# One-hot tables made in two halves, late squares held back, and a new order behind the search

## The chip, the cores and the metric

The kernel runs on one core of one Trainium2 chip. The metric is the device time of one execution in microseconds (us); the kernel before has a median of 389.44 us over 3 runs (389.33 to 390.71). A core has TensorE (PE, matmuls), VectorE (DVE), ScalarE (ACT), GpSimd (POOL) and SyncE (SP, which only issues DMAs here). Each engine runs its own instruction list in the order in which it is written; semaphores tie the lists together.

## The reference

1024 tokens (4 batches of 256) of width 256 pass through four residual blocks:

```
x = x + cross_attention(layernorm(x), ctx)                       # L0_xattn
x = x + turbo_ffn(layernorm(x), w_fc, w_proj)                    # L0_ffn
x = x + smooth_quant_experts(layernorm(x), fside, ctx)           # L1_xattn
x = x + product_key_ffn(layernorm(x), Wq, keys, e_down, e_up)    # L1_ffn

# turbo_ffn: the weights are quantised in blocks of 64. For each block 16 shrink factors are tried
# and the one with the least squared error is kept (the search); then relu(x wq_fc^T)^2 wq_proj^T
# smooth_quant (one expert per batch): s = sqrt(amax_x/amax_w); x/s and w*s rounded to int8 by row;
#   h = xq @ wq^T * scales; a = silu(gate) * up; then the same again with ctx as the down weights
# product_key_ffn: q = x Wq (4 heads, 2 halves of 64); per head and half sim = q keys^T, top 8 of 128;
#   top 8 of the 64 sums; index i1*128 + i2, clipped to the 2048 experts by the gather;
#   out = sum of silu(x . e_down[index]) * relu(score) * e_up[index]
```

## The kernel before, in words

**Stages.** The first 147 us are the search over the weights of the second block, 64 units of PE, ACT and DVE work, with the attention block between them. What the change touches lies behind it, from the line `pe.wait_ge(s["wT_e"], 6)` on in the list of TensorE and from the same place in the others. There, on four batches b (0 to 3) of two tiles of 128 tokens each (t = 2b + n, 0 to 7), these steps run:

- `ffn1(i)`, i = 8 to 15 (L590): the rest of the first feed-forward product; `relu(i)` on ACT (L1133) takes it out of PSUM and `square_hidden(i)` on GpSimd (L347) squares it. `ffn2(b, o)` (L736) is the second product, for batch b and output half o; it needs the transposed weights of chunk 2 or 3 (`w_transposed`, L578), and batches 2 and 3 need all sixteen squares. `x2(b)` on DVE (L1845) adds it to x and takes the statistics.
- The quantised expert (names with `c_`), for each batch a long chain between PE, DVE and ACT: `c_x_transposed`, `c_ratio`, `c_root`, `c_factor`, `c_diag`, `c_factors` (L753), `c_round` (L1875 and on), `c_integers`, `c_clip`, `c_quantised_transposed`, `c_first` (L777), `c_h` (L1902), `c_silu` (L1364), `c_a`, `c_a_transposed` (L784), and the same once more with names ending in 2, up to `c_second` (L813) and `x3(b)` (L1946, L1950). Batches 0 and 2 and 3 share PSUM bank 6, batch 1 has bank 7.
- `pre(b)` transposes the tokens; `half_queries` (L833) and `sims(b, n)` (L846) give the similarities; `experts(b, lo, hi)` (L862) computes the product of the tokens with all 2048 rows of e_down, in eight pieces a batch, which `gate` on ACT (L1418) takes out through silu.
- For each tile t, DVE finds the winners: `top8(t)` (L1960, L1966), `pair_top8(t)` (L1971 to L1981), `look_up(t)` (L1986 to L2002), which leaves for every token and slot the row and column of its expert and its coefficient in three bf16 parts, turned into `packT`. `mask(t)` (L2015) compares the row with 32 columns. `one_hots(t)` compares the column with 128 places (`oh`, L2022, 4096 elements a partition) and multiplies the mask with the three parts (`wc`, L2026, 3072 elements).
- `scatter(b, n, half)` (L884) multiplies `oh` with `wc`, 96 small matmuls for each half of 16 groups, into a dense table of coefficients in PSUM. For tiles 0 to 4 `coefficients_out` on ACT (L1410) moves it and `weigh` on GpSimd (L452) multiplies it with the gates; for tiles 5 to 7 `weigh` on DVE (L2044) does both. `up(b, n, lo, hi)` (L898), 16 pieces a tile, multiplies with e_up, and `result(t)` (L2050) adds it to x for the store.

**What sets the order.** Nothing but the written lists: the order of calls at the end of each engine's block. GpSimd's list is `ranks(t)` (L429), `coefficient_parts(t)` (L436 to L440) and `weigh`. Semaphore counts fix who waits for whom; `d_onehot` counts tiles, and `scatter` waits for it in its first half alone.

Of the kernel before, what the change touches and what calls it, by code (L numbers as in the profile page):

```python
# [36 lines left out]
def build(nc, x, ctx_1024, fside, wq0, bq0, wk0, bk0, w_fc, w_proj, wq1, keys, e_down, e_up, out):  # L37
# [23 lines left out]
    with ctx:  # L61
# [142 lines left out]
        def bk2(i):  # L204
# [16 lines left out]
            attT_t attT_e attn_t x1 ln1_var ln1_std ln1_inv ln1 ln2_var ln2_std ln2 x2T_t x2T_e edT_t edT_e  # L221
# [94 lines left out]
        def _(pool):  # L316
# [90 lines left out]

            square_hidden(8)
# [58 lines left out]
            weigh(2, (0, 1))  # L467
            ranks(4)
            weigh(2, (2, 3))
            coefficient_parts(4)  # L470
            weigh(3, (0,))
            ranks(5)
            weigh(3, (1, 2))
            coefficient_parts(5)
            weigh(3, (3,))
            weigh(4, (0, 1, 2))
            ranks(6)
            coefficient_parts(6)
            weigh(4, (3,))
# [5 lines left out]
        def _(pe):  # L485
# [418 lines left out]
            ffn1(8)  # L904
            ffn1(9)
            ffn1(10)
            pe.wait_ge(s["squared"], NU)
            gate_weights_transposed(0)
            pe.wait_ge(s["hsq"], 8)
            ffn2(0, 0)  # L910
            w_transposed(NCH - 1)
            ffn1(11)
            pe.wait_ge(s["wT_e"], 8)
            ffn2(0, 1).then_inc(s["f2_t"], 1)
            ffn1(12)
            ffn1(13)
            c_x_transposed(0)
            ffn2(1, 0)
            c_factors(0)
            ffn1(14)  # L920
            ffn2(1, 1).then_inc(s["f2_t"], 1)
            ffn1(15)
            c_row_scales(0)
            gate_weights_transposed(1)
            c_quantised_transposed(0)
            gate_weights_transposed(2)
            gate_weights_transposed(3)
            c_first(0)
            c_x_transposed(1)
            pe.wait_ge(s["hsq"], 16)  # L930
            ffn2(2, 0)
            c_a_transposed(0)
            ffn2(2, 1, (0,))
            c_factors(1)
            ffn2(2, 1, (1,)).then_inc(s["f2_t"], 1)
            c_factors2(0)
            ffn2(3, 0)
            ffn2(3, 1, (0,))
            c_row_scales(1)
            c_row_scales2(0)  # L940
            c_quantised2_transposed(0)
            c_quantised_transposed(1)
            c_second(0)
            c_first(1)
            ffn2(3, 1, (1,)).then_inc(s["f2_t"], 1)
            pre(0)
            c_a_transposed(1)
# [4 lines left out]
            c_factors2(1)  # L952
            experts(0, 0, 1)
            sims(0, 0)
            experts(0, 1, 3)
            c_row_scales2(1)
            c_quantised2_transposed(1)
            c_second(1)
            c_factors(2)
            experts(0, 3, 5)  # L960
            sims(0, 1)
            experts(0, 5, 6)
            pe.wait_ge(s["c_pre"], 3)
            pre(1)
            experts(0, 6, 7)
            pe.wait_ge(s["d_xT_e"], 2)
            c_row_scales(2)
            c_quantised_transposed(2)
            experts(0, 7, 8)
            c_first(2)  # L970
            scatter(0, 0, 0)
            c_a_transposed(2)
            half_queries(1, 0, 1)
            scatter(0, 0, 1)
            half_queries(1, 1, 2)
            experts(1, 0, 1)
            c_factors2(2)
            experts(1, 1, 3)
            sims(1, 0)
            experts(1, 3, 4)  # L980
            c_row_scales2(2)
            experts(1, 4, 6)
            c_quantised2_transposed(2)
            experts(1, 6, 7)
            c_second(2)
            experts(1, 7, 8)
            scatter(0, 1, 0)
            sims(1, 1)
# [9 lines left out]
            half_queries(2, 0, 1)  # L998
            up(0, 0, 8, 12)
            experts(2, 0, 1)  # L1000
            half_queries(2, 1, 2)
            up(0, 0, 12, 16)
            c_row_scales(3)
            sims(2, 0)
            c_quantised_transposed(3)
            experts(2, 1, 2)
            c_first(3)
            experts(2, 2, 3)
            scatter(1, 0, 0)
            c_a_transposed(3)  # L1010
            up(0, 1, 0, 4)
            experts(2, 3, 4)
            scatter(1, 0, 1)
            up(0, 1, 4, 16)
            c_factors2(3)
            experts(2, 4, 6)
            up(1, 0, 0, 4)
            c_row_scales2(3)
            sims(2, 1)
            c_quantised2_transposed(3)  # L1020
            up(1, 0, 4, 8)
            c_second(3)
            scatter(1, 1, 0)
            experts(2, 6, 8)
            up(1, 0, 8, 16)
            pre(3)
            scatter(1, 1, 1)
            half_queries(3, 0, 2)
            experts(3, 0, 1)
            scatter(2, 0, 0)  # L1030
            sims(3, 0)
            experts(3, 1, 2)
            scatter(2, 0, 1)
            up(1, 1, 0, 4)
            experts(3, 2, 3)
# [12 lines left out]
            scatter(3, 1, 0)  # L1048
            scatter(3, 1, 1)
            up(3, 0, 0, 16)  # L1050
# [4 lines left out]
        def _(act):  # L1055
# [97 lines left out]
            def square(g):  # L1153
# [7 lines left out]
                if g > QF_LATE:  # L1161
                    act.wait_ge(s["edT_t"], EROWS // 2)
# [256 lines left out]

            relu(8)  # L1420
            relu(9)
            relu(10)
            weights_out(NCH - 1)
            relu(11)
            std(0, 2, "ln3")
            relu(12)
            relu(13)
            c_root(0)
            c_diag(0)
            relu(14)  # L1430
            c_integers(0)
            std(1, 2, "ln3")
            c_row_scales_out(0)
            relu(15)
            c_integers_out(0)
            c_silu(0)
            c_root(1)
            c_diag(1)
# [752 lines left out]
```

## Time and profile before

| | |
|---|---|
| median of 3 runs | 389.44 us |
| the profiled execution's own time | 389.69 us |
| its span | 387.9 us |
| PE busy | 342.5 us (88%) |
| DVE busy | 343.1 us (88%) |
| ACT busy | 247.7 us (64%) |
| POOL busy | 99.6 us (26%) |

The span is the time from the first to the last instruction in the trace; the execution's own time has 1.8 us more around it. Busy time is the time in which an engine had an instruction under way. Two engines are busy for 88% of the span, and both have their idle time in other places, so that neither share alone says what a change in one stretch is worth.

### The profile page before, as it was taken

To read this page: it belongs to the slowest core of one execution; us is meant where nothing else is said; L and a number is where in the kernel's file an instruction comes from. 1 tells how busy PE (TensorE), PEld (TensorE's weight loads), DVE (VectorE), ACT (ScalarE), POOL (GpSimd) and SP (SyncE) were. 2 spreads that over 40 slices of the span, in tenths; PEclk is the share of its full clock that TensorE was granted. 3 is DMA by queue.
4 is the path that set the end of the run, shared out by engine and by line. 5 is a ranking of instruction groups with operands and counts; after the bars stand their busy time and mean duration, and the time that the engine had idled before them with its cause. 6 is when DMAs were issued, how large, how long until landed. Compare 5 with 4: busy or idle time off the path is not lost.

```text
span 387.9 us, 8250 instructions
## 1 busy us (share of the span) xinstructions
PE 342.5 (88%) x3222; PEld 250.7 (65%) x3222; DVE 343.1 (88%) x868; ACT 247.7 (64%) x371; POOL 99.6 (26%) x148
## 2 busy tenths in 40 slices
PE   2997898598968969999979889998999999989997
PEld 2454554144423425778978767887888887778876
DVE  4999999999999999368788999999999999999940
ACT  3899999979999982227457797755766654011000
POOL 3010011340660343121001104256424158601000
PEclk9999999869999999999989999999999999999999
DMA  8930000000000007100000000000000000000000
GB/s 254 358 132 2 1 0 2 1 1 0 2 1 0 2 0 235 37 0 3 0 2 0 3 0 3 1 3 2 0 18 14 2 15 4 2 15 2 18 15 27
DMA packets 11142, 11.40 MB, mean 29 GB/s; under 512 B 608, under 2 KB 10592, under 8 KB 11104
## 3 DMA queue, kind: packets, MB, share of 16 engines
q1 hardware_dynamic: 11104, 10.88, 8.8%
q8 instruction: 25, 0.41, 0.5%
q14 instruction: 13, 0.11, 0.1%
HBM read 9.83 MB, written 1.05 MB: 28 GB/s over the span
## 4 chain that ended last, share of the span: by engine, by line
DVE 53%; PE 25%; ACT 10%; issue 8%; DMA 2%; SPq 1%; POOL 0%; DVEq 0%; ACTq 0%
DVE arena L1627 10%; PE pair L898 7%; PE pair L736 5%; DVE i L1966 4%; DVE arena L1617 3%; DVE s L1960 3%; DVE arena L2026 3%; PE pair L590 3%; DVE arena L2022 2%; ACT arena L1167 2%; ACT arena L1164 2%; DVE XN L1552 2%; PE pair L884 2%; DMA arena<-in_L_ffn_keys_dram 2%; DVE pk L1981 2%
## 5 line engine op out<-in xcount | busy, mean ns | idle before, releaser
L1627 DVE TENSOR_REDUCE arena<-arena 128x16 f32<-128x1024 f32 x64 | 75.8, 1207 | 0.0
L862 PE MATMUL pair<-arena,EDT 128*128 128x256 f32 x256 | 60.2, 383 | 0.0
L898 PE MATMUL pair<-EU,arena 128*128 128x256 f32 x256 | 58.4, 382 | 0.6 <-DVE arena L2050 0.6
L898 PEld LDWEIGHTS pair<-EU,arena 128*128 128x128 f32 x256 | 47.9, 190 | 7.4 <-issue 1.0
L862 PEld LDWEIGHTS pair<-arena,EDT 128*128 128x128 f32 x256 | 47.1, 190 | 6.5 <-ACT arena L1418 0.2
L608 PE MATMUL pair<-arena,WQ 128*128 128x512 fp8e4 x112 | 35.8, 403 | 13.8 <-ACT arena L1164 8.8
L620 PE MATMUL pair<-arena 128*128 128x512 fp8e4 x128 | 40.5, 399 | 2.9 <-DVE arena L1617 2.9
L452 POOL TENSOR_TENSOR arena<-arena 128x512 f32<-128x512 f32 x20 | 27.4, 1383 | 45.0 <-ACT arena L1410 45.0
L1150 ACT ACTIVATE arena<-arena,clip_bias 128x1024 fp8e4<-128x1024 f32 x32 | 37.7, 1187 | 0.3 <-PE pair L620 0.3
L1164 ACT ACTIVATE arena<-pair,sq_bias 128x1024 f32<-128x1024 f32 x32 | 36.6, 1145 | 1.3 <-PE pair L620 1.3
L1418 ACT ACTIVATE arena<-pair 128x512 f32<-128x512 f32 x32 | 19.0, 598 | 26.4 <-PE pair L862 26.4
L1167 ACT ACTIVATE arena<-pair 128x1024 f32<-128x1024 f32 x32 | 33.6, 1051 | 1.4 <-PE pair L620 1.1
L347 POOL TENSOR_TENSOR arena<-arena 128x512 f32<-128x512 f32 x16 | 16.9, 1055 | 60.4 <-ACT arena L1133 60.4
L736 PEld LDWEIGHTS pair<-arena 128*128 128x128 f32 x256 | 30.7, 199 | 1.0 <-issue 1.0
L736 PE MATMUL pair<-arena 128*128 128x128 f32 x256 | 31.2, 282 | 0.0
L608 PEld LDWEIGHTS pair<-arena,WQ 128*128 128x128 bf16 x112 | 8.7, 101 | 34.3 <-ACT arena L1164 13.3
L590 PE MATMUL pair<-arena 128*128 128x512 f32 x64 | 29.7, 597 | 0.9 <-ACT arena L1126 0.7
L1410 ACT COPY arena<-pair 128x512 f32<-128x512 f32 x20 | 19.6, 1071 | 9.9 <-PE pair L884 9.9
L620 PEld LDWEIGHTS pair<-arena 128*128 128x128 bf16 x128 | 12.3, 102 | 20.2 <-issue 4.7
L884 PEld LDWEIGHTS pair<-arena 64*128 64x128 bf16 x1536 | 20.2, 93 | 6.5 <-issue 3.5
L884 PE MATMUL pair<-arena 64*128 64x32 bf16 x1536 | 21.7, 173 | 2.2 <-DVE arena L2044 1.3
L1617 DVE TENSOR_SCALAR arena<-arena 128x1024 fp8e4<-128x1024 f32 x32 | 22.2, 697 | 1.1 <-ACT arena L1138 1.1
(200 smaller groups left out, 642.6 us busy)
## 6 DMA issues: line engine op xcount, KB each, us to landing
arena<-in_L_ffn_e_down_dram SPq DMA_DIRECT2D x1, 2048.0 KB, 12.2
EU<-in_L_ffn_e_up_dram SPq DMA_DIRECT2D x1, 2048.0 KB, 9.3
arena<-in_L_ffn_w_fc_dram SPq DMA_DIRECT2D x2, 512.0 KB, 5.3
X<-in_x_dram SPq DMA_DIRECT2D x1, 1024.0 KB, 5.9
arena<-in_L_ffn_w_proj_dram SPq DMA_DIRECT2D x1, 1024.0 KB, 13.7
GUW<-in_fside_BxS2xS_dram SPq DMA_DIRECT2D x1, 1024.0 KB, 12.4
out_dram<-arena SPq DMA_DIRECT2D x8, 128.0 KB, 1.7
CTX<-in_ctx_dram SPq DMA_DIRECT2D x1, 512.0 KB, 4.8
```

Source lines behind the costliest of these rows:

```text
L590: last = pe.matmul(bank[2 + i % 2], W1T[:, k, m * P:m * P + P], xnT[:, k, half * 512:half * 512 + 512], start=(k == 0), stop=(k == 1))
L608: pe.matmul(to[half], stepN[:, j - 2, :], qr[:, (g - 2) % QDEEP, cols[half]], start=False, stop=False, skip_group_check=True)
L620: last = pe.matmul(to[half], stepI[:, j, :], qr[:, g % QDEEP, cols[half]], start=False, stop=True, skip_group_check=kept)
L736: last = pe.matmul(bk2(F2_BANK[b])[:, n, o * P:o * P + P], h2T[:, k, at:at + P], W2T[:, k, o * P:o * P + P], start=(k == 0), stop=(k == HI ...
L862: last = pe.matmul(bk2(4 + i % 2)[:, r, :], EDT[:, k, at:at + P], xT4[:, b % 2, k, :], start=(k == 0), stop=(k == 1))
L884: last = pe.matmul(bank[scatter_bank(t, half) + r][:, g16 * JW:g16 * JW + JW], oh[rows, g // NG, :, g % NG], wc[rows, c, g // NG, :, g % N ...
L898: last = pe.matmul(bk2(7)[:, n, :], PR[:, n, e, :], EU[:, e, :], start=(e == 0), stop=(e == EROWS - 1))
L1150: act.activation(qr[:, g % QDEEP, :], qu[:, g // NS % 2, :], ACT.Relu, bias=clip_bias[:, 0:1], scale=-GRID / STEPS[g % NS], saturate=False ...
L1164: act.activation(qd(g), pair[2 + g % 2][:, :], ACT.Square, bias=sq_bias[:, g % NS:g % NS + 1]).then_inc(s["squared"], 1)
L1167: act.activation(qd(g), pair[2 + g % 2][:, :], ACT.Square).then_inc(s["squared"], 1)
L1617: dve.tensor_scalar(qr[:, g % QDEEP, :], qu[:, g // NS % 2, :], TB_MAX * STEPS[g % NS], GRID / STEPS[g % NS], ALU.min, ALU.mult, saturate= ...
L1627: dve.tensor_reduce(err[:, g // NS % 2, :, g % NS], squares, AX.X, ALU.add).then_inc(s["reduced"], 1)
```

## The change

`one_hots(t)` becomes `one_hots(t, half)`. Each half makes 2048 elements of `oh` in one instruction and its half of `wc` in three, one for each part, of 512 elements; each half counts one up in `d_onehot`. `scatter` waits for its own half, `mask` for both halves of the tile before, and a half of `oh` waits only for the scatter of the same half of the tile before. On GpSimd `square_hidden(8)` and all after it wait for the last dequantisation, which is on DVE. The lists of PE, ACT, DVE and GpSimd behind the search are written in another order. One wait of `square` in the search is left out for four of five buffers, where an earlier wait covers it. The amount of work of PE, ACT and GpSimd is the same.

```diff
@@ GpSimd
+            pool.wait_ge(s["wquant"], NCH)
             square_hidden(8)
@@ GpSimd, behind ranks(0), coefficient_parts(0)
+            ranks(1)
+            coefficient_parts(1)
             weigh(0, (0, 1, 2))
-            ranks(1)
+            ranks(2)
             weigh(0, (3,))
-            coefficient_parts(1)
-            ranks(2)
-            weigh(1, (0, 1))
             coefficient_parts(2)
-            weigh(1, (2, 3))
+            weigh(1, (0, 1, 2, 3))
...
@@ scatter
-                if half == 0:
-                    pe.wait_ge(s["d_onehot"], t + 1)
+                pe.wait_ge(s["d_onehot"], 2 * t + half + 1)
@@ TensorE, behind ffn1(8)
-            ffn1(9)
-            ffn1(10)
             pe.wait_ge(s["squared"], NU)
-            gate_weights_transposed(0)
             pe.wait_ge(s["hsq"], 8)
             ffn2(0, 0)
+            ffn2(1, 0)
             w_transposed(NCH - 1)
-            ffn1(11)
+            gate_weights_transposed(0)
+            gate_weights_transposed(1)
             pe.wait_ge(s["wT_e"], 8)
             ffn2(0, 1).then_inc(s["f2_t"], 1)
+            ffn2(1, 1).then_inc(s["f2_t"], 1)
+            c_x_transposed(0)
+            ffn1(9)
+            ffn1(10)
+            c_x_transposed(1)
...
+            c_row_scales(1)
             c_first(0)
+            c_quantised_transposed(1)
+            c_first(1)
+            c_a_transposed(0)
+            c_a_transposed(1)
             pe.wait_ge(s["hsq"], 16)
             ffn2(2, 0)
+            c_factors2(0)
             ffn2(2, 1, (0,))
+            c_factors2(1)
+            ffn2(3, 0)
...
@@ TensorE, the end
             sims(3, 1)
-            up(1, 1, 4, 16)
-            scatter(2, 1, 0)
-            experts(3, 3, 5)
+            experts(3, 4, 6)
             scatter(2, 1, 1)
-            experts(3, 5, 7)
-            up(2, 0, 0, 4)
+            experts(3, 6, 7)
+            up(2, 0, 0, 16)
             experts(3, 7, 8)
-            up(2, 0, 4, 16)
             scatter(3, 0, 0)
             scatter(3, 0, 1)
             up(2, 1, 0, 16)
             scatter(3, 1, 0)
+            up(3, 0, 0, 4)
             scatter(3, 1, 1)
-            up(3, 0, 0, 16)
+            up(3, 0, 4, 16)
             up(3, 1, 0, 16)
@@ VectorE
-            def one_hots(t):
-
+            def one_hots(t, half):
+
+                o, k = slice(NO // 2 * half, NO // 2 * half + NO // 2), slice(16 * half, 16 * half + 16)
                 if t:
-                    dve.wait_ge(s["d_c_t"], 4 * t)
-                dve.tensor_tensor(oh, iotaI.unsqueeze(1).to_broadcast([P, NO, P, NG]), over(t, 1, P), ALU.is_equal)
+                    dve.wait_ge(s["d_c_t"], 4 * t - 2 + 2 * half)
+                column = packT[:, t % 2, 1, k].rearrange("p (o g) -> p o g", g=NG).unsqueeze(2).to_broadcast(
+                    [P, NO // 2, P, NG])
+                dve.tensor_tensor(oh[:, o], iotaI.unsqueeze(1).to_broadcast([P, NO // 2, P, NG]), column, ALU.is_equal)
                 dve.wait_ge(s["d_mask"], t + 1)
-                parts = packT[:, t % 2, 2:5, :].rearrange("p c (o g) -> p c o g", g=NG).unsqueeze(3).to_broadcast(
-                    [P, 3, NO, JW, NG])
-                dve.tensor_tensor(wc, msk.unsqueeze(1).to_broadcast([P, 3, NO, JW, NG]), parts, ALU.mult
-                                  ).then_inc(s["d_onehot"], 1)
+                for c in range(3):
+                    part = packT[:, t % 2, 2 + c, k].rearrange("p (o g) -> p o g", g=NG).unsqueeze(2).to_broadcast(
+                        [P, NO // 2, JW, NG])
+                    ins = dve.tensor_tensor(wc[:, c, o], msk[:, o], part, ALU.mult)
+                ins.then_inc(s["d_onehot"], 1)
@@ VectorE, the order of the expert stage
+            x2(1)
             c_ratio(0)
+            ln_apply(1, 2, "ln3")
             c_factor(0)
+            c_ratio(1)
+            c_factor(1)
             c_round(0)
+            c_round(1)
...
+            c_clip2(0)
+            c_clip2(1)
             x2(2)
...
@@ VectorE, the end
             top8(7)
+            pair_top8(7)
             weigh(5, (2,))
-            pair_top8(7)
+            one_hots(6, 0)
+            one_hots(6, 1)
             weigh(5, (3,))
-            one_hots(6)
+            result(4)
             look_up(7)
-            result(4)
-            weigh(6, (0,))
+            weigh(6, (0, 1, 2))
             mask(7)
-            weigh(6, (1,))
-            one_hots(7)
-            weigh(6, (2, 3))
+            one_hots(7, 0)
+            weigh(6, (3,))
             result(5)
+            one_hots(7, 1)
             weigh(7, (0, 1, 2, 3))
             result(6)
             result(7)
```

In the expert stage the lists of PE, ACT and DVE now take batches 0 and 1 side by side (`c_factors(0)`, `c_factors(1)`, `c_round(0)`, `c_round(1)` and so on) and batches 2 and 3 one after the other, where before each batch began some steps behind the last.

## Rows read from the trace of the kernel before

**Rows 1.** The page: busy time by engine, and the last chain's shares.

```profile
PE 342.5 (88%) x3222; PEld 250.7 (65%) x3222; DVE 343.1 (88%) x868; ACT 247.7 (64%) x371; POOL 99.6 (26%) x148
DVE 53%; PE 25%; ACT 10%; issue 8%; DMA 2%; SPq 1%; POOL 0%; DVEq 0%; ACTq 0%
```

**Rows 2.** Stretches: us, busy PE, PEld, DVE, ACT, POOL, PE clock, DMA, GB/s.

```profile
266.00:344.00 78.00, 74.95 (x1125) 64.38 (x1124) 75.46 (x243) 42.49 (x66) 33.98 (x38) 1.00 0.03 9
344.00:388.00 44.00, 40.16 (x632) 34.82 (x632) 28.72 (x66) 1.79 (x3) 1.43 (x6) 1.00 0.04 14
sum 244.00, PE 227.64 PEld 192.85 DVE 206.89 ACT 114.35 POOL 64.33; mean PE 22.76 PEld 19.29 DVE 20.69 ACT 11.44 POOL 6.43
```

**Rows 3.** The chain in order of time, its end (start, us, what).

```profile
342.13 2.08 DVE arena L2044 x2
344.26 1.37 PE pair L884 x96
...
351.01 1.73 PE pair L862 x8
...
378.10 7.16 PE pair L898 x32
```

**Rows 4.** Timeline, DVE: one-hot tables and their neighbours (start, us, line).

```profile
226.97 0.42 DVE L1993 TENSOR_TENSOR arena<-arena,i12f 128x512 bf16<-128x512 bf16 x1
...
229.19 0.69 DVE L2015 TENSOR_TENSOR arena<-arena,ctxT 128x1024 bf16<-128x1024 bf16 x1
...
229.80 0.42 DVE L1891 TENSOR_SCALAR arena<-arena 128x1024 bf16<-128x1024 bf16 x1
...
230.13 2.28 DVE L2022 TENSOR_TENSOR arena<-arena,ctxT 128x4096 bf16<-128x4096 bf16 x1
...
232.33 1.75 DVE L2026 TENSOR_TENSOR arena<-arena,ctxT 128x3072 bf16<-128x3072 bf16 x1
...
234.06 0.88 DVE L1902 SCALAR_TENSOR_TENSOR arena<-pair,rsc,arena 128x256 f32<-128x256 f32 x2
```

**Rows 5.** Timeline of GpSimd and DVE at 317 to 321 us: two together.

```profile
316.73 3.05 POOL L452 TENSOR_TENSOR arena<-arena 128x512 f32<-128x512 f32 x1 [3.38 <-ACT arena L1410]
...
318.56 2.83 DVE L2026 TENSOR_TENSOR arena<-arena,ctxT 128x3072 bf16<-128x3072 bf16 x1
```

**Rows 6.** Timeline of GpSimd and DVE at the last quantisation, and DVE's next stage.

```profile
149.24 1.04 POOL L347 TENSOR_TENSOR arena<-arena 128x512 f32<-128x512 f32 x1 [3.57 <-ACT arena L1133]
...
149.56 1.80 DVE L1595 TENSOR_TENSOR arena<-arena 128x1024 f32<-128x1024 f32 x1
...
162.17 0.69 DVE L1845 TENSOR_TENSOR X<-X,pair 128x512 f32<-128x512 f32 x1 [5.53 <-PE pair L736]
```

**Rows 7.** Timeline of PE, 181 to 202 us, the expert stage.

```profile
181.00 0.61 PE L777 MATMUL pair<-arena 128*128 128x256 bf16 x4 [0.22 <-ACT arena L1355]
...
181.88 3.74 PE L736 MATMUL pair<-arena 128*128 128x128 f32 x32
...
185.46 0.38 PE L784 MATMUL pair<-ident,arena 128*128 128x128 f32 x2
...
198.31 0.38 PE L800 MATMUL pair<-identb,arena 128*128 128x128 bf16 x4 [1.31 <-ACT arena L1390]
...
201.12 3.13 PE L736 MATMUL pair<-arena 128*128 128x128 f32 x16
```

**Rows 8.** Busy time by stretch, one us with the clock down.

```profile
201.00:202.00 1.00, 1.00 (x7) 1.00 (x6) 0.97 (x3) 0.00 (x0) 0.00 (x0) 0.50 0.00 0
```

**Rows 9.** Timeline: first similarities, first top 8, first scatter, second top 8.

```profile
211.68 1.16 PE L846 MATMUL pair<-keysT,arena 64*128 64x128 f32 x16
...
213.59 1.68 DVE L1960 MAX8 s<-pair 128x8 f32<-128x128 f32 x8
...
234.14 1.37 PE L884 MATMUL pair<-arena 64*128 64x32 bf16 x96
...
237.95 1.67 DVE L1960 MAX8 s<-pair 128x8 f32<-128x128 f32 x8
```

More of the change, by code:

```diff
@@ L908, in _ @@
-            gate_weights_transposed(0)
-            pe.wait_ge(s["hsq"], 8)
-            ffn2(0, 0)
-            w_transposed(NCH - 1)
+            c_x_transposed(1)
+            gate_weights_transposed(2)
+            gate_weights_transposed(3)
+            c_factors(0)
             ffn1(11)
-            pe.wait_ge(s["wT_e"], 8)
-            ffn2(0, 1).then_inc(s["f2_t"], 1)
+            c_factors(1)
             ffn1(12)
             ffn1(13)
-            c_x_transposed(0)
-            ffn2(1, 0)
@@ L919, in _ @@
-            c_factors(0)
+            c_row_scales(0)
             ffn1(14)
-            ffn2(1, 1).then_inc(s["f2_t"], 1)
+            c_quantised_transposed(0)
             ffn1(15)
[L923 to L927, printed above, removed]
+            c_row_scales(1)
             c_first(0)
-            c_x_transposed(1)
+            c_quantised_transposed(1)
+            c_first(1)
@@ L930, in _ @@
+            c_a_transposed(0)
+            c_a_transposed(1)
             pe.wait_ge(s["hsq"], 16)
             ffn2(2, 0)
-            c_a_transposed(0)
+            c_factors2(0)
             ffn2(2, 1, (0,))
-            c_factors(1)
+            c_factors2(1)
+            ffn2(3, 0)
+            c_row_scales2(0)
             ffn2(2, 1, (1,)).then_inc(s["f2_t"], 1)
[L936 to L940, printed above, removed]
@@ L941, in _ @@
             c_quantised2_transposed(0)
-            c_quantised_transposed(1)
+            c_row_scales2(1)
             c_second(0)
-            c_first(1)
-            ffn2(3, 1, (1,)).then_inc(s["f2_t"], 1)
+            c_quantised2_transposed(1)
+            ffn2(3, 1).then_inc(s["f2_t"], 1)
             pre(0)
-            c_a_transposed(1)
+            c_second(1)
             pe.wait_ge(s["d_xT_e"], 1)
@@ L951, in _ @@
             half_queries(0, 0, 2)
[L952 removed]
             experts(0, 0, 1)
+            c_factors(2)
             sims(0, 0)
[L955 to L962, printed above, removed]
+            experts(0, 1, 4)
             pe.wait_ge(s["c_pre"], 3)
             pre(1)
[L965 removed]
+            sims(0, 1)
             pe.wait_ge(s["d_xT_e"], 2)
             c_row_scales(2)
+            experts(0, 4, 5)
             c_quantised_transposed(2)
[L969 removed]
+            experts(0, 5, 6)
             c_first(2)
+            experts(0, 6, 8)
+            half_queries(1, 0, 2)
+            experts(1, 0, 1)
+            c_a_transposed(2)
+            experts(1, 1, 2)
             scatter(0, 0, 0)
[L972 to L973 removed]
+            experts(1, 2, 3)
+            sims(1, 0)
+            c_factors2(2)
+            experts(1, 3, 4)
             scatter(0, 0, 1)
[L975 to L980, printed above, removed]
+            experts(1, 4, 5)
             c_row_scales2(2)
[L982 removed]
+            experts(1, 5, 6)
             c_quantised2_transposed(2)
[L984 removed]
+            sims(1, 1)
             c_second(2)
[L986 removed]
+            experts(1, 6, 8)
             scatter(0, 1, 0)
[L988 removed]
             pe.wait_ge(s["x3"], 3)
@@ L1462, in _ @@
+            std(0, 2, "ln4")
+            tokens_out(0)
+            c_root(2)
             std(3, 2, "ln3")
+            queries(0, (0,))
+            c_diag(2)
+            queries(0, (1,))
             std(1, 2, "ln4")
-            gate(0, 3, 5)
+            gate(0, 0, 2)
             c_integers(2)
             tokens_out(1)
-            gate(0, 5, 6)
+            gate(0, 2, 4)
             c_row_scales_out(2)
-            gate(0, 6, 7)
             c_integers_out(2)
-            gate(0, 7, 8)
+            gate(0, 4, 8)
@@ L1472, in _ @@
             c_silu(2)
-            coefficients_out(0, (0, 1))
+            queries(1)
+            gate(1, 0, 1)
             c_root2(2)
-            queries(1, (0,))
-            coefficients_out(0, (2, 3))
+            gate(1, 1, 2)
             c_diag2(2)
-            queries(1, (1,))
-            gate(1, 0, 2)
+            coefficients_out(0, (0,))
+            gate(1, 2, 3)
+            coefficients_out(0, (1,))
             c_integers2(2)
-            gate(1, 2, 4)
+            gate(1, 3, 4)
@@ L1492, in _ @@
             queries(2, (0,))
-            gate(1, 7, 8)
             c_integers(3)
@@ L2115, in _ @@
             c_factor(3)
-            top8(3)
-            c_round(3)
             look_up(2)
             mask(2)
+            c_round(3)
+            one_hots(2, 0)
+            top8(3)
+            c_clip(3)
+            result(0)
             pair_top8(3)
-            c_clip(3)
-            one_hots(2)
+            one_hots(2, 1)
             c_h(3)
-            result(0)
-            c_a(3)
-            top8(4)
-            c_ratio2(3)
             look_up(3)
             mask(3)
+            c_a(3)
+            c_ratio2(3)
+            top8(4)
             c_factor2(3)
```

235 lines of the change are left out of this document (115 added, 120 removed).

## The prediction, made before the changed kernel was run

> **What bounds the kernel now.** I read the page first: PE and DVE are each busy for 88% of the span, and the chain that ended last gives 53% to DVE and 25% to PE [rows 1]. That is an average over stages, so the busy time by stretch came next. From 144 us, where the search ends for PE, to the end, PE is busy for 227.6 of 244 us [rows 2]. The last matmul ends at 378.10 + 7.16 = 385.26 us [rows 3], so 2.7 us of the 16.4 idle ones lie behind it, and 13.7 us is all that a new order can take from PE without taking work away. From 266 to 344 us PE has 3.0 us idle and DVE 2.5 [rows 2]: both are full at once, and a delay on either can reach the end.
>
> Third, the chain in order of time. Up to 344 us it runs on DVE; there PE waits for the multiplications of tile 5 (342.13 + 2.08), and from 344.26 us it is PE's own list to the end [rows 3]. So the end is set in two steps: DVE decides when PE can start that scatter, and what PE has left then decides the rest. What PE has left: 385.26 - 344.26 = 41.0 us. A change gains if DVE arrives at tile 5 earlier, or if PE has done more by then.
>
> **The hold, the search and GpSimd.** DVE's scaling at 149.56 takes 1.80 us; GpSimd's square runs until 149.24 + 1.04 = 150.28, so 0.7 us of it is waiting [rows 6]. With the squares held the last dequantisation should end about 2 us earlier (three such instructions). DVE then idles anyhow: its next stage starts at 162.17 after 5.53 us of waiting for PE [rows 6]. In the new order two second products stand ahead of PE's last weight transposition, about 7.2 us (32 matmuls take 3.74 and let the next start after 3.6 [rows 7]), so PE arrives there at about 155.5 us, when either version of the weights is ready. Gain on the path: 0, bounds 0 and 0.7 (one such wait). If this cover were gone, the 2 us would count in full, as a gain. The held squares are late by some us, but PE needs them only behind the first products of batch 2, 25 us later. The waits left out of the search cost an engine nothing that the trace shows: 0.
>
> **The halves.** The mask of 1024 elements starts at 229.19 and its neighbour at 229.80: 0.61 us. The table of 4096 goes from 230.13 to 232.33, 2.20 us, and the one of 3072 from 232.33 to 234.06, 1.73 us [rows 4]. So an element costs (2.20 - 0.61) / 3072 = 0.52 ns and an instruction 0.08 us beside it. A tile had two of these instructions and gets eight, with the same elements: 6 x 0.08 = 0.48 us, for eight tiles 3.8 us of DVE. Upper end: durations laid end to end. Then 2048 elements cost 0.69 + 1024 x 0.52 ns = 1.22 and 512 cost 0.42 (the row of that size [rows 4]), a tile 2 x 1.22 + 6 x 0.42 = 4.96 against 2.28 + 1.75 = 4.03, and eight tiles 7.4 us. Lower end 0, because no element is saved. I take 3.8: the instructions of these rows have no result of their own to wait for, and their starts are nearer together than their durations. Some 0.5 x 3 us of this lies in tiles 5 to 7.
>
> The row says that a DVE instruction adds 0.08 us when the next overlaps it [rows 4]. The Trainium skill (VectorE: DVE Perf Modes, "The TRN2 errata") says that SBUF latency is exposed between instructions and paid for each small one, and measures a fixed term of about 150 cycles at 0.96 GHz, 0.156 us. By that rule, an estimate from its figure, 48 more instructions cost 7.5 us and not 3.8; no row here has such a train of 512-element products.
>
> What the halves give: a scatter can start 2.2 us before its whole table is ready. PE waits for that table once, 0.57 us at 321 us, in a place where GpSimd had held DVE (below). Taken: up to 0.6 us, and room for the order.
>
> **The expert stage, batches 0 and 1 side by side.** I laid the new lists out by hand with the durations of the same calls. Before, PE had 3.74 us of ffn2 between `c_first` (181.00) and `c_a_transposed` (185.46), 4.46 us in all [rows 7]. Now only a transposition and `c_first(1)`, 0.9 us, lie between, and ffn2 comes behind both. Upper bound of the new hole: 3.6 us. The chain itself (c_h, silu, c_a) is some 2.5 us when DVE isn't taken up with other things, so lower bound 1.6. I take 3.1, with the copy of batch 1 in it. With 0.6 + 0.35 + 0.65 us ahead of it (layer norm of batch 1, diagonals, clip of batch 0) PE idles 4.8 us from 161 to 188 us. In exchange the hole at 197 to 200 us (1.31 us at one place [rows 7]) shrinks to 0.4, but some 1.5 us come at `pre(0)` and the transposition behind it. The clock: before, after that thin stretch 16 matmuls take 3.13 us where 32 had taken 3.74 [rows 7], and the granted clock is 0.50, the 1.2 GHz level [rows 8]. That cost 1.3 us. The new hole is at least as thin, so I put the same dip there and nothing more (bounds: 0, and two dips, 2.6).
>
> By this layout the first similarities start 0.9 us later than before once work done in another order is counted (211.68 before [rows 9]; 214.3 now, with 1.7 us of other work ahead). DVE is ahead: it has done 8.0 us more when it starts its first top 8 at 218.9 us, 5.3 us later than the 213.59 of before [rows 9], so 2.7 us. Behind that point DVE is full, and PE has gates and queries of batch 1 as filler where it had idled for 1.2 us: at the first scatter PE has done 7.2 us more and is at 241.0 against 234.14 + 1.37 = 235.5, so 1.7 us ahead; DVE is 2.0 ahead, measured at the second top 8 (237.95 before [rows 9]). The dip takes up to 1.3 us of both. At `c_x_transposed(3)` I have PE and DVE both 2.0 ahead, 0.7 with the full dip.
>
> **From there to tile 5.** DVE has 4 to 5 tiles with 0.48 us more each, -1.9 to -2.4 us. So it reaches `weigh(5, (0, 1))` between 0.4 us earlier and 1.7 later than 342.13 [rows 3]. At the scatter behind it, PE has one piece of `experts` more behind it than before, 1.73 us (8 matmuls [rows 3]), which covers this.
>
> **The tail.** Behind tile 5 my layout has up(5) end at 365.8, the second scatter of tile 7 wait 1.3 us for its table, `up(3, 0, 0, 4)` filling 0.9 us before it, and the last matmul end at 383.8 with DVE on time, at 385.0 with DVE 1.2 us late. The middle of these, 384.4, is 0.9 us before 385.26.
>
> **Meetings of DVE and GpSimd.** A `wc` of 1.75 us took 2.83 when it started at 318.56 inside a GpSimd product (316.73 + 3.05) [rows 4, 5]: 1.1 us. In the trace behind 262 us eight such instructions lose some 7 us together. The new lists move them all. I count a relief of 0.5 us, since shorter DVE instructions get out of the way sooner; bounds: all of it gone, -7, and half as much again, +3.5.
>
> Sum: -0.9 - 0.5 = -1.4 us. The profiled execution took 389.69 us (387.9 and 1.8 around it), so 388.3 of it; it was 0.25 above the median, so the median should come out at 388.0 us.
>
> **Rivals.**
> 1. The order frees more than my layout shows: DVE's lost time to GpSimd falls by half (3.5 us) and PE's idle 13.7 by some more. For it: both engines are full at once from 266 us, so that nearly all of it is worth its full size, and the first top 8 has 2.7 us in hand. Against: nothing in the rows says that meetings get fewer. About -5, 384.5 us.
> 2. The starved expert stage, on the other side. PE has 3.6 us of hole at `c_a_transposed` and a second thin stretch at 202 to 208 us, the clock falls twice, and DVE's top 8 starts on time or late. Price: 3.6 - 3.1 and one dip more, 1.3, and DVE's lead of 2.7 lost, since its chain hangs on PE's factors: about 4.5 on the forecast, 392.5. It decides once PE loses 3 us more than laid out before 209 us. For it: the filler between `c_first` and `c_a_transposed` is gone [rows 7]. Against: a lead of DVE absorbs part of it.
> 3. Small instructions at their full price, 7.4 us instead of 3.8: DVE, without slack from 266 to 344 us [rows 2], is the bound and gives 3.6 us to the end: -1.4 + 3.6 = +2.2, 391.6. Against: the overlap in rows 4.
> 4. The halves do nothing, as a scatter waits in a list where PE has other work anyhow: then only the order counts. This changes the forecast by under 0.6 us and is inside it.
>
> The order of GpSimd and DVE is what the Trainium skill (SBUF — State Buffer, "Who interferes with whom") has as an exclusive lock for two-input DVE instructions against a GpSimd one that reads. Rows 5 and 6 agree: waits of 1.1 and 0.7 us. By that rule a train of eight instructions offers GpSimd six more places to step in; if it did so for 1 us at one tile in two, the time would be 392.0. That result is a form of rival 3, and its share of the chance is in it.
>
> **Chances.** Forecast (385.5 to 390.5) 0.50: of it 0.20 faster by over 0.5%, 0.29 within, 0.01 slower. Rival 1 0.24 (0.22 faster). Rival 2 0.17 (0.15 slower). Rival 3 0.09 (0.05 slower). 0.5% is 1.95 us, about what a measurement here can tell from no change. Faster 0.42, same 0.37, slower 0.21. The range 383.5 to 392.0 leaves out the far ends of rivals 1 and 2, some 2 in 10.
>
> **What would show it.** Right: DVE starts of 512-element products 0.35 us apart; a hole of 2 to 4 us before `c_a_transposed(0)` at 184 to 188 us with a granted clock of 0.5 behind it; first top 8 at about 219 to 220 us; PE without long waits from 230 us; the last matmul at 384 to 385. Wrong: more than 6 us of PE idle before 209 us or a second clock dip (rival 2); 512-element products over 0.4 us apart (rival 3); last matmul before 382 with few DVE instructions stretched (rival 1).

## The result, and the profile after

The change makes the kernel slower. It takes 397.85 us (median of 4 runs, 396.71 to 399.12) where the kernel before took 390.07 us beside it: 1.0198 times as long, 95% interval 1.0155 to 1.0241 (about 2% slower; the interval leaves out 1). The forecast was 388.0 us, its range ended at 392.0. The profiled execution took 398.09 us with a span of 396.3.

The page of the kernel after: busy time by engine, the clock that PE was granted in 40 slices, and the shares of the chain that ended last.

```profile
PE 344.5 (87%) x3222; PEld 252.6 (64%) x3222; DVE 348.6 (88%) x916; ACT 242.1 (61%) x367; POOL 94.7 (24%) x148
...
PEclk9999999999999989999899999999699989999999
...
DVE 45%; PE 34%; ACT 12%; issue 6%; DMA 2%; SPq 1%; POOL 0%; DVEq 0%; ACTq 0%
```

Against [rows 1] PE has 2.0 us more busy time and DVE 5.5 more, and GpSimd 4.9 less. The next fence has the stretches of [rows 2] in the kernel after.

```profile
266.00:344.00 78.00, 72.06 (x1071) 61.12 (x1063) 73.95 (x238) 41.46 (x64) 27.32 (x34) 0.93 0.02 7
344.00:397.00 53.00, 47.95 (x678) 40.88 (x676) 38.82 (x107) 2.39 (x4) 4.00 (x12) 1.00 0.04 14
```

In 266 to 344 us PE had 1071 matmuls under way and not 1125: PE got less done in this stretch. DVE is nearly as busy as before with 238 instructions and not 243, so its instructions were longer. The points of [rows 9], [rows 3] and [rows 7] answer like this in the kernel after (timelines of PE and DVE).

```profile
181.66 0.62 PE L487 MATMUL pair<-identb,arena 128*128 128x128 bf16 x8 [1.41 <-DVE arena L1884]
...
186.76 0.61 PE L774 MATMUL pair<-arena 128*128 128x256 bf16 x4 [1.10 <-ACT arena L1348]
188.94 1.12 PE L781 MATMUL pair<-ident,arena 128*128 128x128 f32 x4 [1.57 <-DVE arena L1901]
189.85 4.62 PE L733 MATMUL pair<-arena 128*128 128x128 f32 x32
...
216.66 1.16 PE L843 MATMUL pair<-keysT,arena 64*128 64x128 f32 x16
...
240.98 1.37 PE L880 MATMUL pair<-arena 64*128 64x32 bf16 x96
```

```profile
220.21 1.65 DVE L1953 MAX8 s<-pair 128x8 f32<-128x128 f32 x8
...
265.16 0.17 DVE L1855 RECIPROCAL sm<-sm 128x2 f32<-128x2 f32 x1
...
352.09 2.03 DVE L2038 TENSOR_TENSOR arena<-pair,arena 128x512 f32<-128x512 f32 x2
```

The first scatter starts at 240.98 us, where the hand layout had 241.0, and the first top 8 at 220.2 against 218.9. The reciprocal of 265.16 us is the last instruction of `c_factor(3)`. It is a point that both kernels have, called the common point from here on, and there they are nearly level: in the kernel before it starts at 265.39.

```profile
265.39 0.17 DVE L1862 RECIPROCAL sm<-sm 128x2 f32<-128x2 f32 x1
```

Then `weigh(5, (0, 1))` starts at 352.09 and not at 342.13 [rows 3], 9.96 us later. From the common point to it the kernel after takes 86.9 us and the kernel before 76.7, so all of the loss lies between these two points. Behind them the kernel after is the quicker one: its last matmul ends at 386.54 + 7.16 = 393.70, 41.6 us after tile 5's first multiplication, where before it was 43.1 us.

```profile
265.30:352.09 86.79, 80.84 (x1132) 68.52 (x1132) 82.29 (x269) 42.63 (x67) 30.31 (x39) 0.94 0.02 7
```

That is the stretch in question in the kernel after, cut at 265.3 us; the same one before, below, has the same matmuls within 7 and ended 10 us sooner.

```profile
265.30:342.13 76.83, 74.69 (x1125) 64.44 (x1126) 74.25 (x245) 42.31 (x66) 34.15 (x39) 1.00 0.02 7
```

DVE is 8.0 us busier in it. The 24 instructions that the halves add there (269 against 245) are worth some 1.5 of them, as a run below shows. The rest can be seen one by one. GpSimd and DVE in the kernel after, 328 to 338 us:

```profile
329.54 2.88 POOL L453 TENSOR_TENSOR arena<-arena 128x512 f32<-128x512 f32 x2
334.72 2.52 POOL L453 TENSOR_TENSOR arena<-arena 128x512 f32<-128x512 f32 x2 [2.30 <-ACT arena L1403]
```

```profile
329.05 2.23 DVE L2020 TENSOR_TENSOR arena<-arena,ctxT 128x512 bf16<-128x512 bf16 x3
331.20 1.25 DVE L1979 TENSOR_SCALAR pab<-pk 128x32 uint32<-128x32 uint32 x1
332.37 0.17 DVE L1980 TENSOR_SCALAR pab<-pk 128x32 uint32<-128x32 uint32 x1
...
334.85 1.21 DVE L1993 TENSOR_TENSOR pack<-isel,hi 128x32 bf16<-128x32 f32 x1
336.09 0.35 DVE L1995 STREAM_TRANSPOSE ctxT<-pack 128x160 bf16<-128x160 bf16 x1
336.54 1.25 DVE L2005 TENSOR_TENSOR arena<-arena,ctxT 128x1024 bf16<-128x1024 bf16 x1
```

GpSimd's two products run from 329.54 to 332.42. DVE's `pab` of 32 elements starts inside them at 331.20 and ends at 332.45, with the product: 1.25 us where its neighbour L1980 takes 0.17. The packing of 32 elements takes 1.21 inside the product of 334.72. Three products of 512 elements take 2.23 us and undisturbed 1.08. I call "blocked" what a DVE or GpSimd instruction takes beyond the shortest run of the same code line with the same shape in these kernels, if it is over 0.12 us. Summed from the common point to `weigh(5, (0, 1))`:

```
                 DVE blocked        GpSimd blocked    weigh(5,(0,1)) starts
before           6.3 us in 7        10.7 us           342.1
after           12.5 us in 14        5.5 us           352.1
```

### The profile page after: what moved, and what is told of

The parts are those of the page before. It is cut to its first block, busy times and chain, and to the rows that moved or that the text cites. A ratio compares the mean times of both kernels' runs of the same rounds, so it can differ in the third digit from the quotient of the medians.

```text
span 396.3 us, 8298 instructions
## 1 busy us (share of the span) xinstructions
PE 344.5 (87%) x3222; PEld 252.6 (64%) x3222; DVE 348.6 (88%) x916; ACT 242.1 (61%) x367; POOL 94.7 (24%) x148
## 4 chain that ended last, share of the span: by engine, by line
DVE 45%; PE 34%; ACT 12%; issue 6%; DMA 2%; SPq 1%; POOL 0%; DVEq 0%; ACTq 0%
PE pair L894 8%; DVE arena L1620 8%; PE pair L733 7%; PE pair L859 5%; DVE arena L2020 3%; DVE arena L2015 3%; DVE i L1959 3%; ACT arena L1157 3%; PE pair L587 3%; ACT arena L1143 2%; ACT arena L1160 2%; DVE arena L1610 2%; DVE s L1953 2%; PE pair L880 2%; DVE XN L1545 2%
## 5 line engine op out<-in xcount | busy, mean ns | idle before, releaser
L894 PE MATMUL pair<-EU,arena 128*128 128x256 f32 x256 | 61.3, 396 | 0.6 <-DVE arena L2044 0.6
L894 PEld LDWEIGHTS pair<-EU,arena 128*128 128x128 f32 x256 | 49.8, 198 | 8.0 <-issue 1.0
L605 PE MATMUL pair<-arena,WQ 128*128 128x512 fp8e4 x112 | 33.5, 381 | 14.6 <-ACT arena L1157 8.8
L617 PE MATMUL pair<-arena 128*128 128x512 fp8e4 x128 | 38.2, 380 | 2.9 <-DVE arena L1610 2.9
L453 POOL TENSOR_TENSOR arena<-arena 128x512 f32<-128x512 f32 x20 | 29.0, 1460 | 40.6 <-ACT arena L1403 40.6
L347 POOL TENSOR_TENSOR arena<-arena 128x512 f32<-128x512 f32 x16 | 16.6, 1042 | 67.2 <-ACT arena L1126 60.0
L587 PE MATMUL pair<-arena 128*128 128x512 f32 x64 | 31.5, 624 | 1.0 <-ACT arena L1119 0.7
L1403 ACT COPY arena<-pair 128x512 f32<-128x512 f32 x20 | 20.4, 1060 | 5.9 <-PE pair L880 5.9
```

Source lines behind the costliest of these rows:

```text
L587: last = pe.matmul(bank[2 + i % 2], W1T[:, k, m * P:m * P + P], xnT[:, k, half * 512:half * 512 + 512], start=(k == 0), stop=(k == 1))
L605: pe.matmul(to[half], stepN[:, j - 2, :], qr[:, (g - 2) % QDEEP, cols[half]], start=False, stop=False, skip_group_check=True)
L617: last = pe.matmul(to[half], stepI[:, j, :], qr[:, g % QDEEP, cols[half]], start=False, stop=True, skip_group_check=kept)
L894: last = pe.matmul(bk2(7)[:, n, :], PR[:, n, e, :], EU[:, e, :], start=(e == 0), stop=(e == EROWS - 1))
```

## The experiments

Ratios stand against the kernel before, run beside each.

**The halves alone.** The kernel before with its tables in halves, every call one_hots(t) made one_hots(t, 0) and one_hots(t, 1) in place.

```diff
-                    pe.wait_ge(s["d_onehot"], t + 1)
+                pe.wait_ge(s["d_onehot"], 2 * t + half + 1)
...
-            one_hots(5)
+            one_hots(5, 0)
+            one_hots(5, 1)
```

> The kernel before with only the tables in two halves (eight DVE instructions a tile, one half behind the other, a count each, scatter waiting for its half); all orders as before. Theory A (the short instructions are the cause: DVE pays for them and GpSimd gets in between them more often, where before it waited behind long ones): DVE blocked by GpSimd for 9 us or more from 265 us to tile 5 (before 6.3), the first weigh of tile 5 at 346 to 349 us, 393 to 396 us in all. Theory B (the order is the cause): 389 to 391.5 us, the blocked time near 6.

Measured: 391.71 us (10 runs, 390.29 to 392.23), ratio 1.0042 (1.0020 to 1.0065), so +1.6 us. `weigh(5, (0, 1))` starts at 344.34, 2.2 us later, after six tiles: 0.37 us a tile. Blocked are 6.4 us, as before. Its tables at 317 us, on DVE:

```profile
317.51 1.23 DVE L2021 TENSOR_TENSOR arena<-arena,ctxT 128x2048 bf16<-128x2048 bf16 x1
318.65 2.20 DVE L2026 TENSOR_TENSOR arena<-arena,ctxT 128x512 bf16<-128x512 bf16 x3
```

Even here a train of three meets a product (2.20 and not 1.08), where a whole table met it in the kernel before as well [rows 5]. Two more do, at 321.96 and about 336 us:

```profile
321.96 2.25 DVE L2026 TENSOR_TENSOR arena<-arena,ctxT 128x512 bf16<-128x512 bf16 x3
```

So three of the seven blocked instructions are now products of a half, 3.3 us together, where one was a whole `wc` before, 1.1 us. Other meetings went in exchange, and the sum of 6.4 us is that of before: the small instructions are hit more often, but by themselves they cost no more than their launch.

**The order alone.** The kernel after with whole tables, the first one made at the first half's place and the second at the second's.

```diff
...
-                dve.tensor_tensor(oh[:, o], iotaI.unsqueeze(1).to_broadcast([P, NO // 2, P, NG]), column, ALU.is_equal)
+                if half == 0:
+                    dve.tensor_tensor(oh, iotaI.unsqueeze(1).to_broadcast([P, NO, P, NG]), every, ALU.is_equal)
...
+                else:
...
+                    dve.tensor_tensor(wc, msk.unsqueeze(1).to_broadcast([P, 3, NO, JW, NG]), parts, ALU.mult
+                                      ).then_inc(s["d_onehot"], 2)
```

> The changed kernel with whole tables (oh in one instruction at the place of the first half, wc in one at the place of the second, scatter waits for both); all orders as in the changed kernel. Theory A: 391 to 394 us, DVE's blocked time between 265 us and tile 5 back from 12.5 to 6 to 8 us and GpSimd's up. Theory B (order): 396 us or more, since the order stays and every first scatter waits for the whole table.

Measured: 422.57 us, ratio 1.0864 (1.0820 to 1.0909). PE's waits, the first one (us in total, times, longest):

```profile
PE pair L880 <- DVE arena L2020: 26.5, 7, 6.2
```

The new lists put other work between the halves, and a whole table is then complete only behind it. The 26.5 us of PE's waits are those of a table that comes late, so this kernel doesn't tell what the order costs with the tables that it was made for. It shows that the new order can't do without the halves. One of its numbers bears on the cause all the same: from the common point (271.4 us here) to tile 5 DVE has 6.7 us blocked in 8 instructions, about as in the kernel before, though in a stretch with long waits of both engines. Neither the halves alone nor the order alone shows the 12.5 us of the kernel after; what each adds to the other is not separated by these runs.

**Filling PE's hole.** The kernel after with `result(0)` ahead of `top8(3)`, so that eight pieces (16 matmuls) of `up` can stand in front of `c_quantised_transposed(3)`.

```diff
@@ TensorE
+            up(0, 1, 0, 8)
             c_quantised_transposed(3)
...
-            up(0, 1, 0, 4)
...
-            up(0, 1, 4, 12)
+            up(0, 1, 8, 12)
@@ VectorE
+            result(0)
             top8(3)
             c_clip(3)
-            result(0)
```

> The changed kernel with two moves: result(0) ahead of top8(3) on DVE, and eight pieces of up(0, 1) ahead of c_quantised_transposed(3) on PE, where PE stood idle for 2.6 us at 279 us and its clock fell to 0.5. DVE as the bound: the hole and the dip go, and with them DVE's wait of 1.6 us for c_a_transposed(3); 395.5 to 396.5 us. If PE's lost time at this place is itself the loss: 5 us, 393 us.

Measured: 397.96 us, ratio 1.0201 (1.0174 to 1.0227), as after, above both of the expected times. The hole went to the next handover, `c_a_transposed(3)` (PE's waits over the whole kernel; one of the two is the 1.6 us in the expert stage of batches 0 and 1):

```profile
PE pair L781 <- DVE arena L1901: 4.5, 2, 2.9
```

`weigh(5, (0, 1))` starts at 353.2 and DVE has 12.5 us blocked. Filling this hole gives nothing; the runs with small products below show that PE's holes follow from a late DVE.

**No hold of the squares.**

```diff
-            pool.wait_ge(s["wquant"], NCH)
             square_hidden(8)
```

> The changed kernel without the hold of the late squares on GpSimd. Theory: no work of the path hangs on it, 397.4 to 398.4 us, the last quantisation on DVE 0 to 2 us slower and covered by PE's second products. Rival: the squares push the last dequantisation past 155 us and delay PE, 399 us or more.

Measured: 397.07 us (395.06 to 399.01), ratio 1.0169 (1.0132 to 1.0206). Its interval overlaps that of after, and tile 5 and the blocked time (12.6 us) are as there. DVE's last dequantisation and what follows it in the kernel after:

```profile
148.56 0.69 DVE L1596 TENSOR_SCALAR arena<-arena 128x1024 fp8e4<-128x1024 f32 x1
149.29 1.23 DVE L1603 TENSOR_TENSOR arena<-arena 128x1024 f32<-128x1024 fp8e4 x1
```

Without the hold the first of these takes 1.52 us. The hold takes 0.8 us off DVE, in front of an idle time, and is worth nothing to the end.

**Front and back.** Two kernels made of both. Every engine's list is cut at `c_x_transposed(3)`, about 260 us. The first has the new lists and halves up to the cut and the old lists and whole tables behind it; the second the other way round.

```diff
@@ VectorE behind the cut, the first of the two against the kernel after
+            top8(3)
+            c_round(3)
             look_up(2)
             mask(2)
-            c_round(3)
-            one_hots(2, 0)
-            top8(3)
-            c_clip(3)
-            result(0)
             pair_top8(3)
+            c_clip(3)
+            one_hots(2, 0)
             one_hots(2, 1)
...
```

> The changed kernel's lists up to the transposition of batch 3's third norm (about 260 us), with its halves for tiles 0 and 1 and the hold; from there the lists and the whole tables (tiles 2 to 7) of the kernel before. At that cut all four lists have the same calls behind them but for one piece of gate. Theory C (the loss is the order behind the cut): 389 to 391 us, the first weigh of tile 5 on DVE at 342 to 344 us. Rival (the front builds up a debt that shows later): 394 us or more.

> The other half: the lists and the whole tables of the kernel before up to the same cut, the changed kernel's lists with halves for tiles 2 to 7 behind it. Theory C: 396 to 399 us, the first weigh of tile 5 at 351 to 353 us. Rival: 392 us or less.

Measured: the new front 391.20 us (10 runs), ratio 1.0009 (0.9972 to 1.0046); the new back 397.65, ratio 1.0175 (1.0116 to 1.0233). From the cut to tile 5 the first has 6.3 us blocked in 7 DVE instructions, the second 12.6 in 14: the numbers of before and after. The loss is in the back, and the starved expert stage costs nothing that can be told from zero.

**GpSimd's products made small.** In both kernels each of GpSimd's 20 products was cut from 512 elements to 16; the rest of the gates of tiles 0 to 4 is left out.

```diff
-                    pool.tensor_tensor(w, w, gv[:, :, 2 * r:2 * r + 2, 16 * half:16 * half + 16], ALU.mult
+                    pool.tensor_tensor(w[:, 0:1, 0:1], w[:, 0:1, 0:1],
+                                       gv[:, 0:1, 2 * r:2 * r + 1, 16 * half:16 * half + 16], ALU.mult
```

> The kernel before with GpSimd's 20 products of weigh cut from 512 elements a partition to 16 (the rest of the gates is left out for tiles 0 to 4). Theory D (DVE waiting for GpSimd is what costs): its blocked time between 265 us and tile 5 falls from 6.3 to 2 to 4 us, 385 to 388 us in all. Rival (GpSimd's products don't matter to the time): 389 to 390 us.

> The changed kernel with the same cut of GpSimd's products. Theory D: DVE's blocked time falls from 12.5 to 3 to 6 us and with it the time by 6 to 9 us, 389 to 392 us; its distance to b_light is 3 to 5 us and not 8. Rival (the holes of PE and its clock are the cause): the distance to b_light stays 7 us or more, 393 us or more.

Measured: before 384.81 us (0.9844, 0.9786 to 0.9902), after 385.06 us (0.9852, 0.9793 to 0.9912). DVE has nothing blocked in either from 262 us to tile 5, and the difference between the kernels goes from 7.8 us to 0.25. Both lie below what was expected, since all of the blocked time went and not a part. This points at GpSimd's products beside DVE. It leaves one rival: small products are also ready sooner for PE. The runs of the next group, which do all of the work, rule it out. The stretch of [rows 2] in the kernel after with small products:

```profile
266.00:344.00 78.00, 77.96 (x1171) 66.86 (x1163) 74.78 (x290) 41.77 (x63) 14.28 (x39) 1.00 0.03 9
```

PE has no hole left in it, and the clock stands at 1.00, where after had 0.93. So those holes came from DVE's delay.

**The products at times when DVE doesn't mind.** All work done, only GpSimd's list changed. DVE's MAX8 and FIND_INDEX8 and its reductions are nowhere stretched by more than 0.06 us in these traces. So the products are held until DVE comes to a top 8. In the kernel after:

```diff
-            weigh(1, (0, 1, 2, 3))
+            weigh(1, (0,))
+            pool.wait_ge(s["d_onehot"], 5)
+            weigh(1, (1, 2, 3))
             ranks(3)
             coefficient_parts(3)
-            weigh(2, (0, 1, 2))
+            pool.wait_ge(s["c_ratio2"], 4)
+            weigh(2, (0, 1))
             ranks(4)
             coefficient_parts(4)
-            weigh(2, (3,))
+            weigh(2, (2, 3))
+            pool.wait_ge(s["ln4"], 4)
             weigh(3, (0, 1, 2, 3))
             ranks(5)
             coefficient_parts(5)
+            pool.wait_ge(s["d_onehot"], 11)
             weigh(4, (0, 1, 2, 3))
```

> The changed kernel with another list for GpSimd only: its products of tiles 1 to 4 are held (by waits on counts that DVE raises anyway) until DVE begins a top8, whose instructions read PSUM or one operand and were never seen stretched. All work is done. Theory D: DVE's blocked time between 265 us and tile 5 falls from 12.5 to 3 to 6 us, the first weigh of tile 5 comes at 343 to 346 us, 389 to 392 us in all. Rival (holding the products makes up wait for them, or the loss isn't the meetings): 396 us or more.

Measured: 386.35 us (9 runs, 385.06 to 388.02), ratio 0.9916 (0.9884 to 0.9948), so 11.5 us less than the median of the kernel after (11.0 by the two ratios; the two were timed beside different runs of the kernel before), and below the expected 389 to 392. GpSimd and DVE at the last two holds:

```profile
311.06 5.00 POOL L453 TENSOR_TENSOR arena<-arena 128x512 f32<-128x512 f32 x4 [14.23 <-DVE XN L1550]
...
326.28 5.23 POOL L453 TENSOR_TENSOR arena<-arena 128x512 f32<-128x512 f32 x4 [6.68 <-DVE arena L2025]
```

```profile
319.07 1.15 DVE L2025 TENSOR_TENSOR arena<-arena,ctxT 128x512 bf16<-128x512 bf16 x3
320.14 0.17 DVE L1984 TENSOR_SCALAR pab<-pk 128x32 uint32<-128x32 uint32 x1
...
322.69 0.19 DVE L1998 TENSOR_TENSOR pack<-isel,hi 128x32 bf16<-128x32 f32 x1
...
323.37 0.69 DVE L2010 TENSOR_TENSOR arena<-arena,ctxT 128x1024 bf16<-128x1024 bf16 x1
...
326.12 1.67 DVE L1958 MAX8 s<-pair 128x8 f32<-128x128 f32 x8
```

These are the calls that took 2.23, 1.25, 1.21 and 1.25 us in the kernel after. Four products in a row start with the top 8 of 326.12, which takes no longer for them. From the common point to tile 5 DVE has 2.0 us blocked in 3 instructions. That point lies at 263.39 here (this execution came to it 1.8 us earlier) and the multiplication at 338.41: 75.0 us, where after took 86.9. With all of the work done, the loss goes with the meetings: this shows the cause.

The same idea in the kernel before, with two waits:

```diff
+            pool.wait_ge(s["d_final"], 5)
...
-            weigh(3, (0,))
+            weigh(3, (0, 1))
...
-            weigh(3, (1, 2))
+            weigh(3, (2,))
...
-            weigh(4, (0, 1, 2))
+            pool.wait_ge(s["d_mask"], 6)
+            weigh(4, (0, 1, 2, 3))
...
-            weigh(4, (3,))
```

> The kernel before with the same idea: GpSimd's last two products of tile 2 wait for the pair's max, two of tile 3 come before ranks(5), the four of tile 4 wait for mask(5) and so fall into top8(6). Theory D: blocked time 6.3 to 2 to 4 us, 386.5 to 388.5 us. Rival: 390 us.

Measured: 386.62 us (9 runs), ratio 0.9907 (0.9881 to 0.9934), blocked 1.8 us. A last one adds to it the piece of `experts(3)` ahead of tile 5's second scatter:

```diff
-            experts(3, 3, 5)
+            experts(3, 3, 6)
             scatter(2, 1, 1)
-            experts(3, 5, 7)
+            experts(3, 6, 7)
```

> b_quiet, and on PE one more piece of experts (3, 5) ahead of the second scatter of tile 5, where PE waited 1.26 us for DVE, as the changed kernel's tail has it. Theory: PE's own list sets the time from there, so 1 us less than b_quiet, 385.5 to 387.5 us. Rival (DVE sets the tail too): the same as b_quiet.

Measured: 385.95 us (10 runs, 384.49 to 388.76), ratio 0.9918 (0.9882 to 0.9953). Against the one without it, 0.7 us lower in the median, and the spreads overlap: unclear. All three take 0.8 to 0.9% less than the kernel before, with intervals that leave out 1, and none of them is told from another.

## Why the prediction was wrong, step by step

**The step that failed** is "Meetings of DVE and GpSimd", the term "I count a relief of 0.5 us, since shorter DVE instructions get out of the way sooner". Measured, it is 12.53 - 6.27 = +6.3 us before tile 5, beyond the bound of +3.5. I had seen that these meetings cost some 7 us behind 262 us (measured 7.4: 6.3 and 1.1 at 262.72) and that the new lists move all of them. I took the sum of before as a property of the work, and it is one of the timing. Both engines together lose 17.0 us before and 18.0 after. What changed is who waits: GpSimd lost 10.7 and then 5.5, DVE 6.3 and then 12.5. Only DVE's part reaches the end. A bound of "half as much again" had no reason. A sounder upper bound was in the trace of before: GpSimd issues 14 products of 1.28 us in this stretch (15 in the kernel after), and a meeting costs DVE at most about 1.1 us, so by this estimate up to 15 us against 6.3 already paid: +9, not +3.5.

The Trainium skill (SBUF — State Buffer, "Who interferes with whom") says that issue order, not the shape of the operation, decides who blocks, and by that rule a new order reopens the whole account. The trace agrees: a DVE instruction of 32 elements lost 1.1 us. My own rival of this form, 392.0 us by a product stepping into the trains of small instructions, named the right pair of engines and half of the way in. Of the 14 blocked instructions of after, 4 are in such trains (three products of 512 elements and one half of `oh`, 4.1 us), where a whole table lost 1.1 us before: 3.0 of the 6.3 us. The other 3.3 us are in instructions that both kernels have. And the trains alone don't make the loss, since the kernel with halves in the old order has 6.4 us blocked.

**The halves.** Forecast 0.48 us a tile by 0.08 us an instruction, measured 0.37 (2.2 us over six tiles). The overlap held, with starts of 512-element products 0.35 us apart. Rival 3 fell, and so did the fixed 0.156 us an instruction of the estimate from the Trainium skill (VectorE: DVE Perf Modes, "The TRN2 errata"), which would have made it 0.94 us a tile.

**The expert stage and the search.** Right in the main, and the best part of the layout: from 161 to 188 us PE idles 4.6 us (laid out 4.8), with holes of 1.41, 1.10 and 1.57 us at 180 to 189 us. The one directly in front of `c_a_transposed(0)` is 1.57 us and not the 2 to 4 of the sign; with the 1.10 before `c_first(1)` it is 2.7 (laid out 3.1). Then comes a dip of the clock. Over 190 to 193 us the granted clock was 0.72, below the full 2.4 GHz for part of it, and 32 matmuls took 4.62 us instead of the 3.74 of [rows 7]. First top 8 1.3 us late and first scatter on time. Rival 2 fell: the new front alone measures 1.0009. But the lead of 0.7 to 2.0 us at `c_x_transposed(3)` was not there; at the common point, a few us behind it, the kernel after was 0.2 us ahead. The forecast also has a slip here: 2.0 less 1.9 to 2.4 us gives an arrival at tile 5 at most 0.1 us earlier, not 0.4. The start of the first top 8 differs by up to 3.6 us between profiled executions with the same front (211.3 to 214.9), so one pair of traces can't place this lead. The timed runs can: the new front alone is worth between -1.1 and +1.8 us, and the gain of 0.9 that the forecast took is not excluded. It is not the miss.

**The holes behind 230 us.** I expected PE without long waits. It has two:

```profile
277.34 1.37 PE L880 MATMUL pair<-arena 64*128 64x32 bf16 x96
281.31 1.03 PE L487 MATMUL pair<-identb,arena 128*128 128x128 bf16 x8 [2.60 <-DVE arena L1884]
282.13 3.73 PE L894 MATMUL pair<-EU,arena 128*128 128x256 f32 x8
```

```profile
282.00:284.00 2.00, 2.00 (x9) 1.64 (x7) 1.93 (x13) 1.62 (x2) 1.14 (x4) 0.50 0.20 70
```

PE waits 2.60 us for `c_clip(3)`, which stands behind `top8(3)` in DVE's list, then runs at 0.50, the 1.2 GHz level, and 8 matmuls of `up` take 3.73 us. The next hole is 2.84 us, in front of `pre(3)`. DVE in turn waited 1.8 us more than before for PE, 1.6 of it at `c_a_transposed(3)`. These are the wake of DVE's delay: with small products they are gone, and the first one, filled with other work, only moved.

**The sum.** 6.3 (blocked), 1.5 (halves of four tiles) and 1.8 (DVE's waits for PE) are 9.6 of the 9.96 us from 265.3 us to tile 5; 0.4 stays unassigned. The tail gives back 1.5, as laid out, which leaves 8.4; the profiled execution was 8.4 us above 389.69, and the medians differ by 7.8.

**The rest.** The hold: free, as forecast, though 0.8 us of DVE and not 2. "What the halves give" was right in kind: without them the new order costs 25 us more.

## What to carry to other kernels

Where DVE is full and GpSimd works beside it, a reordering draws the meetings of the two anew: bound that term by the number of GpSimd's operations times the most that one meeting cost, not by what the old order happened to pay. Sum the stretched instructions of DVE by form before judging an order, and pin GpSimd's long operations by waits to places where DVE runs instructions that are never stretched; here that was worth some 11 us to one order and 3.1 to the other, and left no difference between the two that could be measured. Shrinking a suspected disturber in both kernels is a cheap first test of such a cause.

## What was not expected of the hardware

- A GpSimd product of 512 elements holds small DVE instructions as long as large ones: `pab`, 32 elements, took 1.25 us instead of 0.17, and the packing 1.21 instead of 0.19. A `wc` of 3072 elements lost 1.1 us too. GpSimd's small ones lose as much to DVE: in the kernel after a CAST of 32 elements took 1.19 us (328.01), where undisturbed it takes 0.21.
- The Trainium skill (SBUF — State Buffer, "Who interferes with whom") says that a DVE instruction with at most one SBUF input and outside the two-port modes doesn't contend with GpSimd. The traces agree: MAX8 and FIND_INDEX8 were never stretched by more than 0.06 us, with four products in a row beside them, nor were the few TENSOR_REDUCE that ran beside a product.
- With the products cut to 16 elements nothing of DVE is blocked, though GpSimd still issues all 20 of them.
